# Moving three one-time jobs in step 2, and a last FFN that takes its high products first

## The reference

```python
x = x + xattn(layernorm(x), ctx)     # q, k, v by 1x1 weights; softmax over 256 keys; plus a skip weight
x = x + ffn(layernorm(x))            # 1024 -> 1024

# ffn: two 4-bit numbers lie in each int32 of qweight (512 x 1024)
low = qweight & 15
high = qweight >> 4 & 15
w_int = jnp.stack([low, high], axis=1).reshape(-1, qweight.shape[1])
zp = jnp.round(zeros / scales)
w = (w_int.astype(jnp.float32) - zp.T) * scales.T
y = x @ w + bias
```

## Time and profile before

| | |
|---|---|
| median of 3 timed runs | 538.35 us (537.58 to 538.68) |
| profiled execution | 536.69 us, its span 534.9 us |
| PE busy | 505.3 us, 94% of the span |
| DVE busy | 429.2 us, 80% |
| ACT busy | 369.7 us, 69% |
| POOL busy | 436.4 us, 82% |
| chain that ended last | POOL 44%, PE 29%, issue 12%, ACT 5%, DVE 5%, DMA 3% |

### The profile page before, as it was taken

How to read it: one execution, slowest core, us unless ns; L and a number is a source line. 1 busy time by engine, 2 the same in 40 slices (tenths; PEclk the granted TensorE clock), 3 DMA queues, 4 the chain that set the end, 5 groups by cost and what they waited for, 6 DMA issues and landing times.

```text
span 534.9 us, 9272 instructions
## 1 busy us (share of the span) xinstructions
PE 505.3 (94%) x2700; PEld 311.9 (58%) x2700; DVE 429.2 (80%) x980; ACT 369.7 (69%) x844; POOL 436.4 (82%) x651
## 2 busy tenths in 40 slices
PE   5657999999999999999999999999999999999976
PEld 4544565656666665666665656666665666665532
DVE  6898788889888888888888889888888888877631
ACT  4877777776777767677777776767767677776510
POOL 5998788889888888988888889888888988888751
PEclk9888999999999999999999999999999999999998
DMA  8636888898788898888898788888897888876852
GB/s 319 172 88 115 144 191 179 179 184 186 168 150 206 188 178 178 181 189 153 178 204 163 193 185 181 157 192 178 172 196 177 194 171 173 163 142 143 154 113 78
DMA packets 236787, 91.65 MB, mean 171 GB/s; under 512 B 219200, under 2 KB 223808, under 8 KB 236736
## 3 DMA queue, kind: packets, MB, share of 16 engines
q1 hardware_dynamic: 236016, 90.92, 79.9%
q10 hardware_dynamic: 720, 0.14, 0.1%
HBM read 23.87 MB, written 16.78 MB: 76 GB/s over the span
## 4 chain that ended last, share of the span: by engine, by line
POOL 44%; PE 29%; issue 12%; ACT 5%; DVE 5%; DMA 3%; SPq 1%; POOLq 0%; ACTq 0%
PE ps_y L907 14%; POOL sb_prob L255 10%; POOL sb_xc_lo L270 9%; POOL sb_xn_lo L297 9%; POOL sb_o L249 6%; PE ps_e L861 5%; PE ps_o L891 4%; ACT sb_xn L487 4%; POOL sb_nb L281 3%; PE ps_o L887 2%; POOL sb_rstd L279 2%; DMA sb_xnt_lo<-sb_xn_lo 2%; POOL sb_rstd L263 2%; PE ps_kv L872 1%; PE ps_y L911 1%
## 5 line engine op out<-in xcount | busy, mean ns | idle before, releaser
L907 PE MATMUL ps_y<-sb_wf,sb_xnt_hi 128*128 128x512 f16 x512 | 196.9, 385 | 7.4 <-DMA sb_xnt_lo<-sb_xn_lo 4.0
L907 PE MATMUL ps_y<-sb_wf,sb_xnt_lo 128*128 128x512 f16 x512 | 196.0, 383 | 0.0
L469 ACT ACTIVATE sb_prob<-ps_e,sb_neg_max 128x256 f32<-128x256 f32 x256 | 117.8, 468 | 53.2 <-DVE sb_neg_max L647 53.2
L255 POOL TENSOR_SCALAR sb_prob<-sb_prob,sb_rsum 128x256 f32<-128x256 f32 x256 | 122.8, 493 | 4.2 <-DVE sb_rsum L652 4.2
L656 DVE TENSOR_TENSOR sb_p_lo<-sb_prob,sb_p_hi 128x1024 f16<-128x1024 f32 x64 | 78.0, 1220 | 48.0 <-ACT sb_p_hi L478 48.0
L297 POOL TENSOR_TENSOR sb_xn_lo<-sb_xn,sb_xn_hi 128x512 f16<-128x512 f32 x64 | 76.0, 1206 | 44.0 <-ACT sb_xn_hi L496 44.0
L861 PE MATMUL ps_e<-sb_k_hi,sb_xc_hi 128*128 128x256 f32 x256 | 85.4, 334 | 10.1 <-DVE sb_k_lo L635 5.5
L907 PEld LDWEIGHTS ps_y<-sb_wf,sb_xnt_hi 128*128 128x128 f16 x512 | 50.2, 98 | 72.8 <-issue 14.1
L478 ACT ACTIVATE sb_p_hi<-sb_prob 128x1024 f16<-128x1024 f32 x64 | 67.3, 1052 | 34.4 <-issue 30.0
L249 POOL TENSOR_TENSOR sb_o<-sb_prod,sb_x 128x512 f32<-128x512 f32 x64 | 80.8, 1281 | 9.5 <-DVE sb_prod L690 9.5
L647 DVE TENSOR_REDUCE sb_neg_max<-ps_e 128x2 f32<-128x512 f32 x128 | 84.8, 681 | 1.6 <-PE ps_e L861 1.2
(11 more groups left out here) (113 smaller groups left out, 917.7 us busy)
## 6 DMA issues: line engine op xcount, KB each, us to landing
sb_x<-in_x_dram SPq DMA_DIRECT2D x32, 512.0 KB, 4.3
out_dram<-sb_o SPq DMA_DIRECT2D x64, 256.0 KB, 2.3
sb_ctx<-in_ctx_dram SPq DMA_DIRECT2D x32, 128.0 KB, 2.8
sb_q<-in_L_ffn_qweight_dram SPq DMA_DIRECT2D x4, 512.0 KB, 7.1
sb_seed_l<-sb_rs SPq DMA_DIRECT2D x96, 0.5 KB, 2.2
sb_pt_hi<-sb_p_hi SPq DMA_TRANSPOSE x64, 4.1
sb_pt_lo<-sb_p_lo SPq DMA_TRANSPOSE x64, 3.4
sb_scale_row<-in_L_ffn_scales_dram SPq DMA_DIRECT2D x1, 512.0 KB, 9.3
```

The lines of the kernel that those rows point to most:

```text
L255: last = pool.tensor_scalar(prob[:, j, t, :], prob[:, j, t, :], rsum[:, j, t:t + 1], P_SCALE, ALU.mult, ALU.mult)
L469: done = act.activation(prob[:, j, t, :], ps_e[j % 2][:, t, :], ACT.Exp, bias=neg_max[:, j, t:t + 1], accum_out=esum[:, j, t:t + 1])
L907: pe.matmul(ps_y[h][:, :], xnt_p[s][:, par, kt, :], wf[:, kt, h * HALF:(h + 1) * HALF], start=kt == 0 and s == 0, stop=False)
```

## The change

In step 2, `nibbles(3)` moves on DVE from behind `values_lo` to ahead of `stats1(4)`; `seed_rows` moves from there to ahead of `stats2(1, 0)`; `turn_seed_rows` moves on PE from behind `scores(2, 1)` and `scores(2, 2)` to ahead of them; `unpack(3)` moves on ACT ahead of `exps(2, 3)`.

For the last block (31) the low half of the split is shared: POOL does the first 512 columns, DVE the others (`last_low`). The transpose of `xn_hi` signals a semaphore of its own, and PE takes the 16 high products of both column halves first, then the low ones and the seed product of half 0, then those of half 1 (`last_ffn`). Its wait for the `seed_l` DMAs now stands ahead of the low products. The last addition (second half of block 31) is done by DVE (`last_out`).

```diff
@@ sync: turn_xn
-                                       xn_hi[:, :, :].rearrange("c k r -> c (k r)")).then_inc(xnt_loaded[par], 16)
+                                       xn_hi[:, :, :].rearrange("c k r -> c (k r)")).then_inc(
+                    last_hi_loaded if a == B - 1 else xnt_loaded[par], 16)
                 sp.wait_ge(xnlo_done, a + 1)
+                if a == B - 1:
+                    sp.wait_ge(last_lo_done, 1)
@@ gpsimd: xn_low, step
-                for k in (0, KT // 2):
+                for k in (0, KT // 2) if a < B - 1 else (0,):
...
                     write_out(c, 0)
-                    write_out(c, 1)
+                    if c < B - 1:
+                        write_out(c, 1)
@@ scalar: step
                     probs_hi(b, 0)
-                    exps(b, 3)
                 if t == 2:
                     unpack(3)
+                if ran(b):
+                    exps(b, 3)
@@ vector
+            def last_low():
+                dve.wait_ge(xnhi_done, B)
+                dve.tensor_tensor(xn_lo[:, KT // 2:, :], xn[:, KT // 2:, :], xn_hi[:, KT // 2:, :],
+                                  ALU.subtract).then_inc(last_lo_done, 1)
+
+            def last_out():
+                cols = slice(HALF, 2 * HALF)
+                dve.wait_ge(prod_done[1], B)
+                dve.wait_ge(stored[(B - 1) % 2], nth(B - 3, 2, 32))
+                dve.tensor_tensor(o_sb[:, (B - 1) % 2, cols], prod[:, 1, :], x1[:, (B - 1) % 3, cols],
+                                  ALU.add).then_inc(out_done[1], 1)
@@ vector: step
                     scale_product(c, 1)
+                if c == B - 1:
+                    last_out()
...
                     value_scale(n)
+                if t == 2:
+                    nibbles(3)
...
                     row_max(b, 2)
+                if t == 2:
+                    seed_rows()
...
-                if t == 2:
-                    nibbles(3)
-                    seed_rows()
...
                     scale_product(q, 0)
+                if a == B - 1:
+                    last_low()
@@ tensor
+            def last_ffn():
+                q = B - 1
+                for s in range(2):
+                    if s == 0:
+                        pe.wait_ge(last_hi_loaded, 16)
+                    else:
+                        pe.wait_ge(xnt_loaded[q % 2], nth(q, 2, 32) - 16)
+                        pe.wait_ge(rs_loaded[q % 2], nth(q, 2, 48))
+                    for h in range(HALVES):
+                        if s == 0:
+                            ffn_ready(q, h)
+                        for kt in range(KT):
+                            ffn_product(q, h, s, kt)
+                        if s == 1:
+                            ffn_terms(q, h)
@@ tensor: step
-                if ran(b):
-                    scores(b, 1)
-                    scores(b, 2)
                 if t == 2:
                     turn_seed_rows(0)
                     turn_seed_rows(1)
+                if ran(b):
+                    scores(b, 1)
+                    scores(b, 2)
...
-                if ran(q):
+                if q == B - 1:
+                    last_ffn()
+                elif ran(q):
```

More of the change, by code:

```diff
@@ L123, in xattn_ffn_program @@
         nb2_done, xn_done, xnhi_done, xnlo_done = (sem(n) for n in ("nb2", "xn", "xnhi", "xnlo"))
+        last_lo_done, last_hi_loaded = sem("last_lo"), sem("last_hi_loaded")
         rshi_done, rs3_done = sem("rshi"), sem("rs3")
@@ L893, in skip_attend, with ffn_product, ffn_terms, ffn_ready @@
                 last.then_inc(attn_done[h], 1)
+            def ffn_product(q, h, s, kt):
+                pe.matmul(ps_y[h][:, :], xnt_p[s][:, q % 2, kt, :], wf[:, kt, h * HALF:(h + 1) * HALF],
+                          start=kt == 0 and s == 0, stop=False)
+            def ffn_terms(q, h):
+                pe.matmul(ps_y[h][:, :], seed_l[:, q % 2, :], seed_row[:, h * HALF:(h + 1) * HALF],
+                          start=False, stop=True).then_inc(y_done[h], 1)
+            def ffn_ready(q, h):
+                if ran(q, 1):
+                    pe.wait_ge(prod_done[h], q)
+                else:
+                    pe.wait_ge(rows_done, 2)
             def ffn(q, h):
@@ L906, in ffn @@
                     for s in range(2):
-                        pe.matmul(ps_y[h][:, :], xnt_p[s][:, par, kt, :], wf[:, kt, h * HALF:(h + 1) * HALF],
-                                  start=kt == 0 and s == 0, stop=False)
+                        ffn_product(q, h, s, kt)
                 if h == 0:
                     pe.wait_ge(rs_loaded[par], nth(q, 2, 48))
-                pe.matmul(ps_y[h][:, :], seed_l[:, par, :], seed_row[:, h * HALF:(h + 1) * HALF],
-                          start=False, stop=True).then_inc(y_done[h], 1)
+                ffn_terms(q, h)
[4 more added lines that the diff above has]
+                        pe.wait_ge(last_hi_loaded, 16)
+                    else:
+                        pe.wait_ge(xnt_loaded[q % 2], nth(q, 2, 32) - 16)
+                        pe.wait_ge(rs_loaded[q % 2], nth(q, 2, 48))
+                    for h in range(HALVES):
+                        if s == 0:
+                            ffn_ready(q, h)
+                        for kt in range(KT):
+                            ffn_product(q, h, s, kt)
+                        if s == 1:
+                            ffn_terms(q, h)
             def keys_ready(b):
@@ L947, in step @@
                     skip_attend(a, 0)
+                if t == 2:
+                    turn_seed_rows(0)
+                    turn_seed_rows(1)
                 if ran(b):
@@ L950, in step @@
                     scores(b, 2)
-                if t == 2:
-                    turn_seed_rows(0)
-                    turn_seed_rows(1)
                 if ran(a):
```

## The result

The changed kernel takes 532.17 us (median of 4 runs, 531.56 to 532.22) against 538.03 us (4 runs, 537.58 to 538.68) for the kernel before beside it: a ratio of 0.989 [0.9876, 0.9904], 5.9 us less. The forecast was 532.0.

A forecast was written before the change was run, and what follows sets the result against it. PE's own work and a POOL-ACT loop, nearly equal per step, were taken to bound the kernel. Step 2's -1.8 and the end's -4.6 us made -6.4, from 538.35 to 532.0 us; range 530.4 to 534.2 for 8 times in 10.

The forecast's parts named there:

- term 1: Step 2: PE 2.5 us earlier, the loop over POOL and ACT 1.8 us earlier; -1.8 us counted at the end.
- Term 2: The end: -3.97 us from PE's stop and clock, -0.6 from the last addition on DVE; -4.6 us.
- the bound from exclusion: Last low half: if DVE and POOL exclude each other, sharing saves only 0.5 us, not up to 1.19.
- the prediction's list of what holds the first FFN: Step 2 on PE: two jobs, the seed-row copies ending at 50.78 us and `unpack(3)` ending at 54.95.
- The loop: POOL to ACT and back, 15.409 us a step against PE's 15.374; predicted to gain 1.8 us in step 2.
- The term of 0.75: Step 2: `xn_low(1)` on POOL starts 0.75 us earlier, the middle between bounds 0 and 1.5.
- a gain in step 2 counts at the end only as far as the loop is earlier too: Ordinary steps: PE alone being earlier would be waited back at `xnt_lo`, so only the loop's 1.8 us counts.
- PE's whole lead counts: Rival, step 2: the loop follows PE by 2.5 us, 7.1 us saved in all, 531.2 us; chance 0.15.
- The clock did not fall behind the new stop: Rival, step 2: the clock falls at PE's stop ahead of kt = 6; 5.4 us saved, 533.0; chance 0.15.
- Step 2 gives nothing: Rival: the loop is held by something moved later; only 4.6 us saved, 533.8 us; chance 0.1.
- the end gives less: Rival: high transpose lands late or the clock falls anyway; half of 3.97 us, 534.0 us; chance 0.06.
- slower: Rival: DVE's two-input operations fall on POOL's in each step; at 0.3 us a step, 540.4 us; chance 0.04.

The follow-up runs named there:

- no shared low: The changed kernel with `xn_low(31)` wholly on POOL again, the last addition staying on DVE; 531.81 us, 0.9905 of the kernel before.
- Step 2 only: The kernel before with the edits of step 2 alone, the end as before; 534.81 us, 0.9939 of the kernel before.
- end only: The kernel before with the three edits at the end alone, step 2 as before; 534.34 us, 0.9928 of the kernel before.
- unpacking stays: The changed kernel with `unpack(3)` back behind `exps(2, 3)`; 534.10 us, 0.9917 of the kernel before.
- before again: The kernel before, unchanged, run again for a second profile and the scatter; 538.12 against 538.47 us, 0.999.
- nibbles stay: The changed kernel with `nibbles(3)` back behind `values_lo`, the seed copies staying early; 532.19 us, 0.9914 of the kernel before.
- order only: The kernel before with only the new order of PE's last products; low half and last addition stay on POOL; 534.92 us, 0.9933 of the kernel before.
- early out but last: The changed kernel with POOL writing out a half FFN ahead of `xn_low`, except for block 30; 531.01 us, 0.9865 of the kernel before.

## Why the prediction was right, step by step

The forecast of 532.0 met 532.17, and that it came so close is partly luck. The same kernel saved 5.9 us in one set and 7.2 in another, and inside term 1 several sizes were off in opposite directions. What the runs bear out is the mechanism of both terms, with the one correction under "what reaches the end".

**Term 2, the end: -4.6 predicted, -4.7 in the tail, -4.1 timed alone.** The last seed product starts 14.45 us after FFN(30) in place of 18.51: -4.06 against the predicted -3.97. The stop and the clock went as said. The condition was that the seeds land by 522.3; the low products started at 522.37, straight behind the 16 high ones. Sharing the low half saves 0.5 us of SP's wait, as the bound from exclusion said: from the issue of `xnt_hi` to that of `xnt_lo` there are 1.83 us in the changed kernel and 2.34 both before and with "no shared low". DVE's half took 1.58 us beside POOL's 1.16. The rule of the Trainium skill that the prediction weighed ("SBUF — State Buffer", Who interferes with whom) agrees with these rows in the main: DVE's half, started 0.12 us behind POOL's, ended 0.54 us behind the end of POOL's, where such an operation takes 0.69 us by itself. The last addition was worth 0.64, against 0.6.

**Term 1, step 2: -1.8 predicted; the sum was a little small.** The unchanged step 2 (first four rows of the table) has FFN(30) at 473.6 on average. The four profiles with the whole of the new step 2 (both of the changed kernel, and the two variants of its end) have 471.35: -2.3. "Step 2 only", where x landed 1.2 us late, has 472.94; with it the mean gain is 1.9. The two profiles at the head of this part give only 1.27, since "before" is 0.8 to 1.1 us ahead of the other three with the old step 2. Timed, the changed kernel is at -5.9 and -7.2 in its two sets and "end only" at -4.1, so step 2 gives 1.8 to 3.1; alone it gave 3.6.

- PE: the first score product of step 3 is 2.45 us earlier (21.83 to 19.38 on average), predicted 2.5. In the first two profiles alone it is 2.07, and the product at kt = 6 is earlier by the same 2.06. Inside that, two sizes were off against each other. `probs_hi(2, 0)` starts 11.56 us after the key product in place of 10.93, so 0.6 us later, where I allowed 0.2: the reciprocal behind the seed copies. Mostly for this reason the stop ahead of kt = 6 is 1.86 us in place of 1.3 (that 12 x 0.21 is 2.5 and not 2.6 changes nothing). And kt = 6 had a second holder that I had not seen, the half clock, under which the twelve products ended only at 55.00. By these rows, and this is an argument and not a run, the unpacking moved alone would have met PE still at half clock. The copies and nibbles moved without it are "unpacking stays", where step 3 gained nothing. So the unpacking's move is shown to be needed and that of the copies argued, and the prediction's list of what holds the first FFN had only two of the three entries.
- The loop: `xn_low(1)` is 0.45 us earlier on average (20.15 to 19.70), where I took 0.75 between bounds of 0 and 1.5. The wait ahead of `normalise(3, 0)` went as said, and that operation starts 1.6 us earlier, predicted 1.8. The term of 0.75 was too large, since `normalise(2, 3)`, which the chain to `xn_low(1)` goes through, took 1.83 us beside DVE, in place of the 0.93 of two such halves at 64.37.
- What reaches the end, 2.3, lies between the loop's 1.6 and PE's 2.45. My step "a gain in step 2 counts at the end only as far as the loop is earlier too" was too strict, and the loop's step was not 15.41 us, which I had put among the signs of being wrong: it is 15.42 to 15.45 in the changed kernel's two profiles, and 15.45 in "before again", so this is no effect of the change. PE's median step is 15.37 in every profile. It is PE's own work that fills the time to FFN(30), and what a late loop takes back is a few short waits. PE, 60 to 509 us, before:

```profile
60.00:509.00 449.00, 448.20 (x2442) 1.00 0.85 176
```

After:

```profile
60.00:509.00 449.00, 447.85 (x2436) 1.00 0.84 176
```

PE stands for 0.8 us in the one and for 1.15 in the other. So most of PE's own lead does count, as the rival "PE's whole lead counts" had it.

**The rivals.** The clock did not fall behind the new stop of 1.86 us; that it can in this place is shown at 2.95 us ("unpacking stays"), and that it need not at 2.12 ("nibbles stay"). "Step 2 gives nothing" is excluded by "end only" against the changed kernel, "the end gives less" by the tail. The lengthening that "slower" feared is there: DVE's `wsk_lo`, with two inputs from SBUF, takes 605 ns before and 1139 ns in the changed kernel. That is not the change alone, since "order only", whose step 2 is the old one, has 945. Before (DVE, 60 to 480 us: busy, mean ns):

```profile
L640 DVE SCALAR_TENSOR_TENSOR sb_wsk_lo<-sb_proj,sb_sk_scale,sb_wsk_hi 128x128 fp32r<-128x128 f32 x27 | 16.3, 605 | 0.0
```

After:

```profile
L646 DVE SCALAR_TENSOR_TENSOR sb_wsk_lo<-sb_proj,sb_sk_scale,sb_wsk_hi 128x128 fp32r<-128x128 f32 x27 | 30.8, 1139 | 0.0
```

It costs nothing that the rows show: DVE waits 44.7 us for `p_hi` in the same stretch, and 44.5 before. In "early out but last", where POOL's writing out has moved, it takes 418 ns.

**Left open:** what would bound the last steps once `xnt_lo` and `pt_lo` come in time; why the half level of the clock in the run-in lasts longer in some executions than in others; and why the load of block 4 lands anywhere from 3.8 to 5.3 us behind the key product.

## What to carry to other kernels

Look at the granted clock behind each long stop before you move work into or out of it: a stop that is shortened in front and comes back in the middle of a burst of products can cost all that was won, and one that ends up short enough gives the clock back as well. At a drain, put the products whose operand is there first, and check by the rows that the rest lands within their length. And when an edit takes one of several holders away, measure from a mark in the same run, since the two spans here differed by 1.45 us before the changed code began. Even then look at what stands at the mark and just behind it: here the clock and one load still differed, and shifted the marks of step 2 by up to 1 us.

## What the runs showed of the hardware

- The granted clock in a window of 2 us behind a stop of PE: 0.53 behind 3.42 us, 0.50 behind 2.95 us, 0.62 behind 2.29 us; 1.00 behind 2.12 us ("nibbles stay") and behind 1.86 us. These are single places, not a limit.
- Small GpSimd operations next to DVE's int32 nibbles: POOL's L295 on 128x1 took 0.72 us beside them and 0.19 in "step 2 only", where it came behind them, as the 1.10 us in the earlier trace rows had suggested.
- The landing of one load of 512 KB: the statistics that wait for it start 4.03 us behind the key product before, 4.16 in the changed kernel and 5.33 in "step 2 only".
